# A state-space recurrence with the shared expert's matmuls between its units: x1 is turned four units earlier, and the last shared block gets a plan of its own

## The chip, the cores and the metric

The kernel runs on one core of a Trainium2 chip. The metric is the device time in microseconds (us), the median of three runs. On this core TensorE (PE) multiplies matrices into PSUM, VectorE (DVE), ScalarE (ACT) and GpSimd (POOL) work elementwise, and SyncE (SP) issues most DMAs.

## The reference

The input x is 4096 tokens by 512 channels. Two sublayers follow each other, each with a layer norm before it and one after it, and a residual.

```python
xp = x @ W_x;  dt = softplus(xp[:, :64] @ W_dt + b_dt);  B, C = xp[:, 64:80], xp[:, 80:96]
h  = exp(dt * A) * h + (dt * x) * B          # per token, 512 channels x 16 states
y  = sum_n(h * C) + x * D_skip
x1 = x + layernorm(y)
# second sublayer, on xt = layernorm(x1): top 2 of 8 experts with a capacity, and a shared expert
sh = gelu(xt @ sw1 + sb1) @ sw2 + sb2 + gelu(xt @ swd) @ swu
out = x1 + layernorm(sum_k(weight_k * expert_k(xt)) + 0.2 * sh)
```

## The kernel before

There are three program blocks, one after another: `prepare` (norm of x, dt and the B and C tables), `mix` (the recurrence, x1, and the shared expert for most tokens), and `experts` (router, gathered experts, the last 512 tokens of the shared expert, the final norm). The change touches `mix` alone.

**Units and chunks.** `mix` cuts the tokens in 8 chunks of 512 (`NCH`). A chunk has 64 units (`NU`): 4 slices of 128 channels by 16 states. A unit g is a 128x512 step on every engine: POOL makes u = dt*x*B (`drive`, line 897), ACT makes exp(dt*A) in a PSUM bank (`decay`, 646, after the one-column copy `keep`, 635), DVE runs the scan over 512 tokens (`recur`, 790) and multiplies by C (`weigh`, 797), PE adds the product, turned, into `psY` (`add`, 1014; `add_skip`, 1022, at the end of a slice, whose sum ACT takes out with `take`, 655). From unit 117 on only two PSUM banks serve the decays, so ACT makes the decay of unit g+2 in its iteration g, after the product of unit g. POOL's u runs up to six units ahead, and the products may lie five units ahead of PE.

**What is laid between the units.** When a chunk is over, its y is normed and x is added by two DMAs (`norm`, 659, units 5 to 8 of the next chunk; `residual`, 922, units 8 and 10), which gives x1. Then DVE takes the statistics of x1 (unit 16), POOL the inverse deviation (17), ACT norms four tiles (`norm_x1`, 667), SP stores them (`store_xt`, 573). PE turns each tile (`turn`, 1033) into the PSUM bank `psH`, ACT rounds it (`x_hi`, 676), DVE makes the rest (`x_lo`, 822), and each turn waits for the rest of the tile before. Then the shared expert of these 512 tokens, block b: 17 W1 blocks (`up`, 1050, twelve matmuls each; number 0 is the low-rank and router part), each taken out of the one bank `psH` by ACT two units later (`hidden_out`, 691), four bursts of gelu (`gelus`, 700, with a change of ACT's table before and after), `h_hi` (ACT, 715) and `h_lo` (POOL, 906), and 17 W2 blocks (`down`, 1071, twelve matmuls; number 0 has four, line 1061) into four PSUM banks, which DVE empties (`shared_out`, 841).

**What sets the order.** The order is a table of units, written out by hand. `due(b, unit)` gives the unit of the whole run at which a step of block b is issued; each engine walks over all units g and issues what is due, in program order, and semaphores hold the data together. A block's plan is longer than a chunk: W1 blocks at units 37, 40, ... 85 and W2 blocks at units 59 to 112, so units 0 to 21 of a chunk have W1 blocks of the block before, units 1 to 48 its W2 blocks. The recurrence has 512 units and block 6, the last in it, starts in the last chunk; what is due after unit 63 of that chunk runs without a recurrence beside it, and so do the turns and block 0 of W1 for the last 512 tokens. POOL issues the load of W1 block j+3 four units after W1 block j (950), and W2 likewise (959).

Of the kernel before, what the change touches and what calls it, by code (L numbers as in the profile page):

```python
# [36 lines left out]
FC = FF // P  # L37
# [327 lines left out]
BT = 4  # L365
FB = T // (BT * P) - 1
L3 = 3 * LR
T_AT, X_HI_AT, X_LO_AT = (24, 27, 31, 34), (25, 29, 32, 35), (27, 31, 34, 37)
UP_AT = tuple(37 + 3 * j for j in range(J))
BURST_AT = (52, 64, 77, 90)  # L370
HI_AT = (56, 58, 68, 74, 83, 88, 94, 101)
LO_AT = (59, 62, 71, 77, 86, 93, 98, 104)
LOW_HI_AT, LOW_LO_AT = 55, 58
DOWN_AT = (59, 62, 65, 68, 71, 74, 78, 81, 84, 87, 90, 94, 97, 99, 102, 106, 112)
OUT_AT = 119
B_FREE, C_FREE = 45, 51
FIRST = min(T_AT)
END = (NCH + 1) * NU
# [5 lines left out]
def due(b, unit):  # L384

    return (b + 1) * NU + unit


def mix(nc, sem, const, early, x, dt_d, dtx_d, bc_d, xT_d, w, ws_d, lgT_d, x1_d, xt_d, sh_d):
# [6 lines left out]
    with ExitStack() as ctx:  # L396
# [129 lines left out]
        @block.sync  # L526
        def _(sp):
            def next_pass(s):
                after(sp, s_yc, s - 1)
                load_pass(sp, dt_d, dtx_d, early, s)  # L530

            def next_skip(s):
                after(sp, s_yc, s)
                load_skip(sp, xT_d, early, s)

            def used(c, j):
                return (c - 1) * NU + (DT - 1) * NS + (j + 1) * TG

            def next_B(c, j):
                sp.wait_ge(s_u, used(c, j))  # L540
                load_table(sp, bc_d, Bt, s_B, 0, j, c)

            def next_C(c, j):
                sp.wait_ge(s_pd, used(c, j))
                load_table(sp, bc_d, Ct, s_C, NS, j, c)

            def load_raw(i):
                after(sp, s_wl, i - 3)
                if i < FC // 2:
                    f = 2 * i * P  # L550
                    sp.dma_start(raw_columns(i), w["sw1"].rearrange("(a p) f -> p a f", p=P)[:, :, f:f + 2 * P])\
                        .then_inc(s_wr[i % 4], 16)
                else:
                    r = (2 * i - FC) * P
                    sp.dma_start(raw_pair(i), w["sw2"][r:r + 2 * P, :].rearrange("(o p) d -> p o d", p=P))\
                        .then_inc(s_wr[i % 4], 16)

            def store_lo(i):
                sp.wait_ge(s_wl, i + 1)
                sp.dma_start(split_rows(i, 1), halves(hl, i).bitcast(F32)).then_inc(s_wls[i % 2], 16)  # L560

            def rows(a, c, t):
                return a[c * CH + t * P:c * CH + (t + 1) * P, :]

            def store_x1(c):
                for o in range(2):
                    sp.wait_ge(s_x1[o], (c + 1) * 16)
                sp.dma_start(x1_d[c * CH:(c + 1) * CH, :].rearrange("(t p) d -> p t d", p=P), ys[c % 2][:, :, :])\
                    .then_inc(s_out, 16)

            def store_xt(b, t):
                sp.wait_ge(s_xn, b * BT + t + 1)
                sp.dma_start(rows(xt_d, b, t), xn[t % 2][:, :]).then_inc(s_xt[t % 2], 16)

            def store_sh(b, t):
                sp.wait_ge(s_yev, b * BT + t + 1)
                sp.dma_start(rows(sh_d, b, t), yst[t][:, :]).then_inc(s_sh[t], 16)

            def store_logits(b):
                sp.wait_ge(s_ev, b * J + 1)  # L580
                sp.dma_start(lgT_d[:, b * CH:(b + 1) * CH], g0[L3:L3 + E, :]).then_inc(s_lgs, 16)

            sp.dma_start(wd_raw, w["swd"].rearrange("(a p) n -> p a n", p=P)).then_inc(s_stat, 16)
            sp.dma_start(gate_raw, w["gate"].rearrange("(a p) e -> p a e", p=P)).then_inc(s_stat, 16)
            for k in range(3):
                sp.dma_start(wu_raw[k * LR:(k + 1) * LR, :], w["swu"]).then_inc(s_stat, 16)
            for i in range(4):
                load_raw(i)
            sp.dma_start(b2bc[:, :], w["sb2"].partition_broadcast(P)).then_inc(s_bias, 16)
            for g in range(END):  # L590
                c, k = g // NU, g % NU
                if g == 40:
                    with nc.allow_non_contiguous_dma(reason="2048 biases"):
                        sp.dma_start(b1T[:, :], w["sb1"].rearrange("(c p) -> p c", p=P)).then_inc(s_bias, 16)
                if g == 20:
                    sp.wait_ge(early["s_last"][0], NCH // 2 * 16)
                    sp.wait_ge(early["s_last"][1], NCH // 2 * 16)
                if g % SPLIT == 0 and 0 < g // SPLIT <= FC:
                    store_lo(g // SPLIT - 1)
                    if g // SPLIT + 3 < FC:  # L600
                        load_raw(g // SPLIT + 3)
                if g % NS == 2 and 0 < g // NS < PASSES - 1:
                    next_pass(g // NS + 1)
                if g % NS == 4 and 0 < g // NS < PASSES:
                    next_skip(g // NS)
                for j in range(NG):
                    if c + 1 < NCH and k == B_FREE + 2 * j:
                        next_B(c + 1, j)
                    if 0 < g - C_FREE - 2 * j < UNITS - NU and (g - C_FREE - 2 * j) % NU == 0 or g == C_FREE + 2 * j:
                        next_C((g - C_FREE - 2 * j) // NU + 1, j)  # L610
                if c > 0:
                    if k == 16:
                        store_x1(c - 1)
                    if k in (20, 23, 29, 32):
                        store_xt(c - 1, (20, 23, 29, 32).index(k))
                for b in blocks(g):
                    for t in range(BT):
                        if due(b, OUT_AT) + 1 + t == g:
                            store_sh(b, t)
                for b in turned(g):  # L620
                    if due(b, UP_AT[0]) + 4 == g:
                        store_logits(b)
            sp.wait_ge(s_out, 16 * NCH)
            for q in range(2):
                sp.wait_ge(s_xt[q], (FB + 1) * BT // 2 * 16)
            for t in range(BT):
                sp.wait_ge(s_sh[t], FB * 16)
            sp.wait_ge(s_lgs, (FB + 1) * 16)

        @block.scalar  # L630
        def _(act):
# [106 lines left out]
            for g in range(END):  # L738
# [16 lines left out]
                if c > 0:  # L755
                    if k in (5, 6, 7, 8):
                        norm(c - 1, k - 5)
                    if k in (18, 21, 27, 30):
                        norm_x1(c - 1, (18, 21, 27, 30).index(k))
                for b in turned(g):  # L760
                    for t in range(BT):
                        if due(b, X_HI_AT[t]) == g:
                            x_hi(b, t)
                    if due(b, UP_AT[0]) + 2 == g:
                        hidden_out(b, 0)
                for b in blocks(g):
                    for j in range(1, J):
                        if due(b, UP_AT[j]) + 2 == g:
                            hidden_out(b, j)
                    for q in range(4):  # L770
                        if due(b, BURST_AT[q]) == g:
                            gelus(b, q)
                    if due(b, LOW_HI_AT) == g:
                        low_rank_hi(b)
                    for i in range(FC // 2):
                        if due(b, HI_AT[i]) == g:
                            h_hi(b, 2 * i + 1)

        @block.vector
        def _(dve):  # L780
# [75 lines left out]
            for g in range(END):  # L856
# [5 lines left out]
                        if due(b, X_LO_AT[t]) == g:  # L862
                            x_lo(b, t)
                for b in blocks(g):
                    if due(b, OUT_AT) == g:
                        for t in range(BT):
                            shared_out(b, t)
                    if due(b, LOW_LO_AT) == g:
# [20 lines left out]
        def _(pool):  # L889
# [70 lines left out]
                                    ws_d[FC + n % FC, :, :, :].rearrange("p h x -> p (h x)")).then_inc(s_w2[k], 16)  # L960

            def free_w1(n):
                return due((n - W1_RING) // FC, UP_AT[(n - W1_RING) % FC + 1]) + 4

            def free_w2(n):
                return due((n - W2_RING) // FC, DOWN_AT[(n - W2_RING) % FC + 1]) + 4

            def load_first():
                pool.wait_ge(s_yc, PASSES)
# [10 lines left out]
            for g in range(END):  # L980
# [5 lines left out]
                for b in blocks(g):  # L986
                    for i in range(FC // 2):
                        for o in range(2):
                            if due(b, LO_AT[i]) + o == g:
                                h_lo(b, 2 * i + 1 + o)  # L990
                if c > 0 and k == 4:
                    inverse(c - 1)
# [14 lines left out]
        def _(pe):  # L1007
# [68 lines left out]
            for g in range(END):  # L1076
# [4 lines left out]
                for b in turned(g):  # L1081
                    for t in range(BT):
                        if due(b, T_AT[t]) == g:
                            turn(b, t)
                    if due(b, UP_AT[0]) == g:
                        up(b, 0)
                for b in blocks(g):
                    for j in range(J):
                        if j > 0 and due(b, UP_AT[j]) == g:
                            up(b, j)  # L1090
                        if due(b, DOWN_AT[j]) == g:
                            down(b, j)


# [1143 lines left out]
```

## Time and profile before

| | |
|---|---|
| median of three runs | 3402.59 us (3400.78 to 3402.65) |
| span of the profiled execution | 3388.4 us |
| around the span (median less span) | 14.2 us |
| first scan of the recurrence | 151.7 us from the span's start |
| last product of the recurrence | 1306.4 us |
| last matmul of `mix` | ends 1377.9 us |

The profile is of one execution. Its span goes from the first to the last instruction; its own device time is not listed apart from the runs, so the span is put beside their median. PE is busy for 91% of it. The recurrence fills 151.7 to 1306.4 us; a chunk takes 146.7 to 149.8 us from chunk 2 on. 1306.4 to 1377.9 is the tail of `mix`, in which the shared expert's blocks that are left run alone; `experts` follows to the end. Times in the text are us from the span's start unless said otherwise.

### The profile page before, as it was taken

The page shows a single profiled execution, that of the slowest core. Times are in us where ns is not written, and L with a number is a line of the kernel's source. Part 1 is how long each engine was busy: PE and PEld are TensorE (multiplying, and loading weights), DVE is VectorE, ACT ScalarE, POOL GpSimd, SP SyncE. Part 2 cuts the span into 40 slices and gives each one's busy share as a digit, 9 for nine tenths or more (in the row PEclk, how much of TensorE's full clock was granted, in tenths as well). Part 3 has the DMA queues.
Part 4 walks back from the last instruction along what each step waited for, and adds up shares of the span by engine and source line. Part 5 has one row for each costly group of instructions (what it writes and reads, how often), then busy time and mean ns, then how long its engine had stood idle before and what let it go on. Part 6 is the DMA issues. An engine that isn't in the chain of part 4 may idle for free.

```text
span 3388.4 us, 42962 instructions
## 1 busy us (share of the span) xinstructions
PE 3100.0 (91%) x15139; PEld 2538.6 (75%) x15139; DVE 1812.1 (53%) x2476; ACT 1633.6 (48%) x2978; POOL 1384.2 (41%) x1367
## 2 busy tenths in 40 slices
PE   6464799988989899999999999999999999999997
PEld 3243677777767777788888888888888888888886
DVE  7797989988998984441331332322313313313345
ACT  7654676666767665452332432433423424324343
POOL 2297787988988785311110121021111111211224
PEclk9655899999999999999999999999999999999999
DMA  7968678696977865930320420412312303204355
GB/s 265 303 189 250 163 229 217 203 268 183 257 192 225 230 190 186 288 95 19 88 69 13 106 60 16 119 37 54 97 20 75 78 16 100 63 10 115 75 184 161
DMA packets 273447, 466.30 MB, mean 138 GB/s; under 512 B 30817, under 2 KB 102193, under 8 KB 273234
## 3 DMA queue, kind: packets, MB, share of 16 engines
q1 hardware_dynamic: 200400, 264.91, 26.5%
q0 software_dynamic: 66720, 189.87, 21.3%
q10 hardware_dynamic: 6114, 8.79, 0.7%
q8 instruction: 121, 1.98, 0.2%
q14 instruction: 92, 0.75, 0.1%
HBM read 366.33 MB, written 97.16 MB: 137 GB/s over the span
## 4 chain that ended last, share of the span: by engine, by line
PE 53%; DMA 2%; DVE 2%; issue 1%; ACT 1%; POOL 0%; SPq 0%; POOLq 0%; DVEq 0%; ACTq 0%
PE c_psH L2030 26%; PE c_psY L2071 25%; PE c_psT L2021 1%; DMA out<-d_y 1%; PE c_psY L2067 0%; DVE yst L1734 0%; DMA raw<-in_w 0%; DMA W2l<-ws_d 0%; DVE hl L1754 0%; ACT h L1487 0%; DVE hl L1759 0%; DVE wgt L1923 0%; PE c_psT L2130 0%; DVE hh L1753 0%; DMA d_x1p<-x_d 0%
## 5 line engine op out<-in xcount | busy, mean ns | idle before, releaser
L1759 DVE TENSOR_TENSOR hl<-h,hh 128x512 fp32r<-128x512 f32 (+1 forms) x400 | 242.5, 606 | 1185.3 <-ACT hh L1491 1185.2
L1489 ACT ACTIVATE h<-c_psH,biases 128x512 f32<-128x512 f32 (+1 forms) x400 | 248.1, 620 | 1045.0 <-PE c_psH L2030 1033.0
L897 POOL TENSOR_TENSOR u<-dtxs,Bt 128x512 f32<-128x512 f32 x512 | 669.3, 1348 | 148.2 <-DVE b_psA L790 132.9
L790 DVE TENSOR_TENSOR_SCAN b_psA<-b_psA,b_few,u 128x512 f32<-128x512 f32 x473 | 606.4, 1282 | 75.0 <-ACT b_psA L646 74.0
L2071 PE MATMUL c_psY<-W2h,hh 128*128 128x512 f32 x1344 | 535.2, 398 | 1.8 <-DVE hl L1759 1.1
L1014 PE MATMUL b_psY<-ident,pr 128*128 128x128 f32 x2048 | 345.7, 308 | 208.2 <-DVE pr L797 190.1
L2071 PE MATMUL c_psY<-W2l,hh 128*128 128x512 f32 x1344 | 525.4, 391 | 0.0
L2071 PE MATMUL c_psY<-W2h,hl 128*128 128x512 f32 x1344 | 524.4, 390 | 0.0
L1567 POOL DMA_INDIRECT xrow<-xt_d,slot_lists x80 | 84.7, 1059 | 1050.3 <-PE c_psT L2021 600.2
L1014 PEld LDWEIGHTS b_psY<-ident,pr 128*128 128x128 f32 x2048 | 265.9, 156 | 290.8 <-DVE pr L797 238.7
L646 ACT ACTIVATE b_psA<-dts,wgt 128x512 f32<-128x512 f32 x473 | 327.4, 692 | 14.9 <-ACT b_few L635 0.2
L797 DVE TENSOR_TENSOR pr<-b_psA,Ct 128x512 f32<-128x512 f32 x473 | 325.5, 688 | 14.4 <-DMA Ct<-bc_d 0.7
L1050 PE MATMUL b_psH<-Xh,w 128*128 128x512 f32 x896 | 316.7, 415 | 9.9 <-DMA w<-ws_d 9.7
L1607 POOL DMA_INDIRECT acc_d<-yst,slot_lists x72 | 117.4, 1630 | 442.7 <-DVE yst L1734 425.3
L2071 PEld LDWEIGHTS c_psY<-W2h,hl 128*128 128x128 f32 x1344 | 252.8, 188 | 54.9
L2071 PEld LDWEIGHTS c_psY<-W2h,hh 128*128 128x128 f32 x1344 | 253.2, 188 | 53.2 <-DVE hl L1759 6.2
L1071 PE MATMUL b_psS<-w,hhs 128*128 128x512 f32 x896 | 292.7, 408 | 0.0
L2071 PEld LDWEIGHTS c_psY<-W2l,hh 128*128 128x128 f32 x1344 | 253.5, 189 | 46.6 <-issue 0.2
L1491 ACT ACTIVATE hh<-c_psH,biases 128x512 fp32r<-128x512 f32 (+1 forms) x400 | 245.1, 613 | 0.0
L2030 PE MATMUL c_psH<-Xh,W1h 128*128 128x512 f32 x576 | 224.5, 390 | 0.7 <-DMA W2l<-ws_d 0.7
L2030 PE MATMUL c_psH<-Xl,W1h 128*128 128x512 f32 x576 | 224.3, 389 | 0.0
L2030 PE MATMUL c_psH<-Xh,W1l 128*128 128x512 f32 x576 | 224.2, 389 | 0.0
(271 smaller groups left out, 5685.1 us busy)
## 6 DMA issues: line engine op xcount, KB each, us to landing
w<-ws_d POOLq DMA_DIRECT2D x224, 512.0 KB, 6.6
raw<-in_w SPq DMA_DIRECT2D x256, 256.0 KB, 2.8
Bt<-bc_d SPq DMA_DIRECT2D x64, 512.0 KB, 14.6
Ct<-bc_d SPq DMA_DIRECT2D x64, 512.0 KB, 19.1
xn<-in_x SPq DMA_DIRECT2D x8, 1024.0 KB, 7.9
xT_d<-xnT SPq DMA_DIRECT2D x8, 1024.0 KB, 12.5
dt_d<-a_dt SPq DMA_DIRECT2D x8, 1024.0 KB, 8.5
dtx_d<-a_dx SPq DMA_DIRECT2D x8, 1024.0 KB, 8.7
```

The source lines that it names most:

```text
L646: nc.scalar.activation(bank(g)[:, :], dts[s % 2][:, :], ACT.Exp, scale=A_neg[:, s % DT, n:n + 1]).then_inc(s_dA, 1)
L790: nc.vector.tensor_tensor_scan(a[:, :], a[:, :], u[g % U_RING][:, :], carry[:, k:k + 1], ALU.mult, ALU.add).then_inc(s_h, 1)
L797: nc.vector.tensor_tensor(pr[g % PR_RING][:, :], bank(g)[:, :], C_of(g), ALU.mult)\
L897: nc.gpsimd.tensor_tensor(u[g % U_RING][:, :], dtx[s % 2][:, :], Bt[n // TG][:, n % TG, :], ALU.mult)\
L1014: last = nc.tensor.matmul(psY[:, t, :], pr[g % PR_RING][:, t * P:(t + 1) * P], ident[:, :], start=(n == 0 and t == 0), stop=False, is_tran ...
L1050: last = nc.tensor.matmul(out, a[:, d, :], v[:, d, :], start=(d == 0 and i == 0), stop=(d == DT - 1 and i == 2))
L1071: last = nc.tensor.matmul(psS[t][:, :], a, v, start=False, stop=(j == FC and i == 2))
L1489: nc.scalar.activation(h32[:, 0:n * P], psH[j % 2][:, 0:n * P], ACT.Gelu, bias=b1[:, j - 1:j])
L1491: nc.scalar.activation(hh[j % 2][:, 0:n * P], psH[j % 2][:, 0:n * P], ACT.Gelu, bias=b1[:, j - 1:j]).then_inc(s_gelu, 1)
L1759: nc.vector.tensor_tensor(hl[j % 2][a], h32[a], hh[j % 2][a].bitcast(F32), ALU.subtract)\
L2030: last = nc.tensor.matmul(out, a, b, start=(i == 0), stop=(i == n - 1))
L2071: last = nc.tensor.matmul(psY[t][:, :], a[j % 2][:, c], b, start=False, stop=(j == J - 1 and i == 2))
```

## The change

The turns of x1 move from units 24, 27, 31, 34 to 20, 23, 27, 30, `x_hi` and `x_lo` with them by four units. The norms before them move from 18, 21, 27, 30 to 18, 20, 23, 26 and the stores from 20, 23, 29, 32 to 19, 22, 25, 28. W1 blocks start at unit 34 instead of 37, still every three units, so their units are the same ones with one more at 34 and none at 85 (unit 21 of the next chunk). Bursts, `h_hi`, `h_lo`, W2 blocks and the output keep their units. Block 6 gets a plan of its own, `FINAL`.

```diff
-T_AT, X_HI_AT, X_LO_AT = (24, 27, 31, 34), (25, 29, 32, 35), (27, 31, 34, 37)
-UP_AT = tuple(37 + 3 * j for j in range(J))
-BURST_AT = (52, 64, 77, 90)
-HI_AT = (56, 58, 68, 74, 83, 88, 94, 101)
-LO_AT = (59, 62, 71, 77, 86, 93, 98, 104)
+T_AT, X_HI_AT, X_LO_AT = (20, 23, 27, 30), (21, 25, 28, 31), (23, 27, 30, 33)
+X1_NORM_AT, XT_STORE_AT = (18, 20, 23, 26), (19, 22, 25, 28)
 LOW_HI_AT, LOW_LO_AT = 55, 58
-DOWN_AT = (59, 62, 65, 68, 71, 74, 78, 81, 84, 87, 90, 94, 97, 99, 102, 106, 112)
-OUT_AT = 119
+USUAL = dict(
+    up=tuple(34 + 3 * j for j in range(J)), burst=(52, 64, 77, 90), hi=(56, 58, 68, 74, 83, 88, 94, 101),
+    lo=(59, 62, 71, 77, 86, 93, 98, 104),
+    down=(59, 62, 65, 68, 71, 74, 78, 81, 84, 87, 90, 94, 97, 99, 102, 106, 112), out=119)
+FINAL = dict(
+    up=(34, 37, 40, 43, 46, 48, 50, 52, 54, 56, 58, 60, 62, 68, 70, 74, 77), burst=(51, 57, 65, 81),
+    hi=(54, 58, 67, 71, 76, 81, 86, 91), lo=(57, 61, 69, 74, 78, 83, 88, 93),
+    down=(62, 64, 66, 68, 70, 73, 75, 78, 80, 83, 85, 88, 90, 92, 94, 97, 99), out=102)
...
+def plan(b):
+
+    return FINAL if b == FB - 1 else USUAL
```

Everywhere else `UP_AT`, `BURST_AT` and so on become `plan(b)["up"]`, `plan(b)["burst"]`. No instruction is added or taken away; the order on each queue changes.

## Rows read from the trace of the kernel before

**Rows 1.** Part 1 of the page: busy us (share of the span) xinstructions
```profile
PE 3100.0 (91%) x15139; PEld 2538.6 (75%) x15139; DVE 1812.1 (53%) x2476; ACT 1633.6 (48%) x2978; POOL 1384.2 (41%) x1367
```
**Rows 2.** Busy time by stretch: chunk 5, chunk 7, tail of mix
```profile
core 0: us, PE busy (x) PEld busy (x) DVE busy (x) ACT busy (x) POOL busy (x), PEclk, DMA share, GB/s
863.84:1010.86 147.02, 133.17 (x707) 110.14 (x707) 133.44 (x155) 99.89 (x187) 124.69 (x123) 0.95 0.80 221
...
1157.55:1306.36 148.81, 133.69 (x713) 110.79 (x712) 133.60 (x154) 99.46 (x186) 121.42 (x120) 0.97 0.62 188
1306.36:1377.90 71.54, 71.53 (x329) 58.66 (x327) 10.58 (x23) 27.99 (x36) 33.26 (x43) 1.00 0.65 202
```
**Rows 3.** Waits within chunk 5: total us, times, longest
```profile
PE b_psY L1014 <- DVE pr L797: 11.2, 9, 4.5
DVE b_psA L790 <- ACT b_psA L646: 7.9, 6, 2.3
```
**Rows 4.** DVE in order of time, chunk 5: start, us, instruction, [idle before]
```profile
918.00 1.29 DVE L790 TENSOR_TENSOR_SCAN b_psA<-b_psA,b_few,u 128x512 f32<-128x512 f32 x1 [0.96 <-ACT b_psA L646]
...
919.93 1.28 DVE L790 TENSOR_TENSOR_SCAN b_psA<-b_psA,b_few,u 128x512 f32<-128x512 f32 x1
...
924.83 1.29 DVE L790 TENSOR_TENSOR_SCAN b_psA<-b_psA,b_few,u 128x512 f32<-128x512 f32 x1 [0.96 <-ACT b_psA L646]
...
928.44 0.69 DVE L822 TENSOR_TENSOR Xl<-b_psH,Xh 128x512 fp32r<-128x512 f32 x1 [1.59 <-ACT Xh L676]
929.04 1.28 DVE L790 TENSOR_TENSOR_SCAN b_psA<-b_psA,b_few,u 128x512 f32<-128x512 f32 x1
...
934.59 1.29 DVE L790 TENSOR_TENSOR_SCAN b_psA<-b_psA,b_few,u 128x512 f32<-128x512 f32 x1 [1.62 <-ACT b_psA L646]
...
945.94 0.69 DVE L822 TENSOR_TENSOR Xl<-b_psH,Xh 128x512 fp32r<-128x512 f32 x1 [1.03 <-ACT Xh L676]
...
986.34 1.29 DVE L790 TENSOR_TENSOR_SCAN b_psA<-b_psA,b_few,u 128x512 f32<-128x512 f32 x1 [0.62 <-ACT b_psA L646]
...
992.22 1.29 DVE L790 TENSOR_TENSOR_SCAN b_psA<-b_psA,b_few,u 128x512 f32<-128x512 f32 x1 [1.48 <-ACT b_psA L646]
```
**Rows 5.** ACT in order of time, around the burst of unit 26
```profile
929.21 1.28 ACT L700 ACT_TABLE_LOAD   x1
930.50 2.01 ACT L700 ACTIVATE hb<-hb 128x1024 f32<-128x1024 f32 x2
...
933.87 0.69 ACT L646 ACTIVATE b_psA<-dts,wgt 128x512 f32<-128x512 f32 x1
934.50 0.80 ACT L667 ACTIVATE xn<-ys,b_few 128x512 f32<-128x512 f32 x1
```
**Rows 6.** PE in order of time, units 30 to 56 of chunk 5
```profile
938.59 1.12 PE L1014 MATMUL b_psY<-ident,pr 128*128 128x128 f32 x4 [0.81 <-DVE pr L797]
...
950.53 0.66 PE L1014 MATMUL b_psY<-ident,pr 128*128 128x128 f32 x4 [0.34 <-DVE pr L797]
...
954.98 0.66 PE L1014 MATMUL b_psY<-ident,pr 128*128 128x128 f32 x4 [0.61 <-DVE pr L797]
955.39 0.47 PE L1050 MATMUL b_psH<-Xh,L1h 128*104 128x512 f32 x1
...
958.25 0.60 PE L1014 MATMUL b_psY<-ident,pr 128*128 128x128 f32 x4
...
994.30 1.11 PE L1014 MATMUL b_psY<-ident,pr 128*128 128x128 f32 x4 [4.52 <-DVE pr L797]
```
**Rows 7.** Busy time and granted clock of shorter stretches, columns as in rows 2
```profile
934.90:941.60 6.70, 4.12 (x13) 3.29 (x14) 6.60 (x8) 5.41 (x12) 5.51 (x5) 0.50 0.37 122
941.70:985.60 43.90, 42.03 (x237) 34.99 (x236) 42.12 (x46) 23.28 (x52) 37.08 (x35) 1.00 0.59 172
...
1281.30:1310.30 29.00, 22.76 (x120) 18.65 (x117) 22.72 (x25) 18.03 (x31) 14.56 (x14) 0.94 0.40 127
```
**Rows 8.** The same view for the tail from unit 64's W1 block on
```profile
1310.30:1377.70 67.40, 67.40 (x307) 55.29 (x305) 10.38 (x23) 27.63 (x35) 32.22 (x41) 1.00 0.66 205
```
**Rows 9.** POOL in order of time: second residual DMA of the tail
```profile
1323.42 1.74 POOL L922 DMA_DIRECT2D ys<-in_x  x1
```
**Rows 10.** ACT in order of time: first norm of x1 in the tail
```profile
1341.12 0.80 ACT L667 ACTIVATE xn<-ys,b_few 128x512 f32<-128x512 f32 x1
```
**Rows 11.** PE in order of time: first turn of the tail
```profile
1353.93 0.60 PE L1033 MATMUL b_psH<-ident,xn 128*128 128x128 f32 x4
```

More of the change, by code:

```diff
@@ L613, in _ @@
                         store_x1(c - 1)
-                    if k in (20, 23, 29, 32):
-                        store_xt(c - 1, (20, 23, 29, 32).index(k))
+                    if k in XT_STORE_AT:
+                        store_xt(c - 1, XT_STORE_AT.index(k))
                 for b in blocks(g):
                     for t in range(BT):
-                        if due(b, OUT_AT) + 1 + t == g:
+                        if due(b, plan(b)["out"]) + 1 + t == g:
                             store_sh(b, t)
                 for b in turned(g):
-                    if due(b, UP_AT[0]) + 4 == g:
+                    if due(b, plan(b)["up"][0]) + 4 == g:
                         store_logits(b)
@@ L757, in _ @@
                         norm(c - 1, k - 5)
-                    if k in (18, 21, 27, 30):
-                        norm_x1(c - 1, (18, 21, 27, 30).index(k))
+                    if k in X1_NORM_AT:
+                        norm_x1(c - 1, X1_NORM_AT.index(k))
                 for b in turned(g):
@@ L763, in _ @@
                             x_hi(b, t)
-                    if due(b, UP_AT[0]) + 2 == g:
+                    if due(b, plan(b)["up"][0]) + 2 == g:
                         hidden_out(b, 0)
@@ L767, in _ @@
                     for j in range(1, J):
-                        if due(b, UP_AT[j]) + 2 == g:
+                        if due(b, plan(b)["up"][j]) + 2 == g:
                             hidden_out(b, j)
                     for q in range(4):
-                        if due(b, BURST_AT[q]) == g:
+                        if due(b, plan(b)["burst"][q]) == g:
                             gelus(b, q)
@@ L775, in _ @@
                     for i in range(FC // 2):
-                        if due(b, HI_AT[i]) == g:
+                        if due(b, plan(b)["hi"][i]) == g:
                             h_hi(b, 2 * i + 1)
@@ L864, in _ @@
                 for b in blocks(g):
-                    if due(b, OUT_AT) == g:
+                    if due(b, plan(b)["out"]) == g:
                         for t in range(BT):
@@ L962, in free_w1 @@
             def free_w1(n):
-                return due((n - W1_RING) // FC, UP_AT[(n - W1_RING) % FC + 1]) + 4
+                b, j = (n - W1_RING) // FC, (n - W1_RING) % FC + 1
+                return due(b, plan(b)["up"][j]) + 4
             def free_w2(n):
-                return due((n - W2_RING) // FC, DOWN_AT[(n - W2_RING) % FC + 1]) + 4
+                b, j = (n - W2_RING) // FC, (n - W2_RING) % FC + 1
+                return due(b, plan(b)["down"][j]) + 4
             def load_first():
@@ L988, in _ @@
                         for o in range(2):
-                            if due(b, LO_AT[i]) + o == g:
+                            if due(b, plan(b)["lo"][i]) + o == g:
                                 h_lo(b, 2 * i + 1 + o)
@@ L1084, in _ @@
                             turn(b, t)
-                    if due(b, UP_AT[0]) == g:
+                    if due(b, plan(b)["up"][0]) == g:
                         up(b, 0)
@@ L1088, in _ @@
                     for j in range(J):
-                        if j > 0 and due(b, UP_AT[j]) == g:
+                        if j > 0 and due(b, plan(b)["up"][j]) == g:
                             up(b, j)
-                        if due(b, DOWN_AT[j]) == g:
+                        if due(b, plan(b)["down"][j]) == g:
                             down(b, j)
```

## The prediction

> **What bounds the kernel now.** I read the busy shares first, then the stages, then the waits of one chunk, then single queues around the moved steps. PE is busy for 91% of the span and DVE for 53% [rows 1], but the change lies in the recurrence, where both are near full: in chunk 5 each has some 133 us of 147.02 [rows 2]. Two scans follow each other in 1.93 us [rows 4], so 64 units need 123.5 us; the rest is other DVE work and idle time. The idle time is divided: DVE waits 7.9 us for ACT's decays, and PE waits 11.2 us for DVE's products [rows 3]. So neither is the bound throughout; they take turns. After the recurrence the tail is PE alone: 71.53 us busy of 71.54 [rows 2]. `experts` starts when `mix` ends, so its part of the span should only shift.
>
> Chunks 2 to 6 show the same pattern, so I price chunk 5 and multiply by five; chunks 1 and 7 and the tail are taken apart.
>
> **Turns four units earlier, up to unit 30.** Before, DVE loses 0.96 us twice (918.00, 924.83: the scans of units 23 and 26 wait for decays that stand behind an eviction of a late W1 block), 1.59 us at the first `x_lo` (928.44), 1.62 us at scan 29 and 1.03 us at the third `x_lo` [rows 4]. That is 6.2 us, the largest prize in sight. Walked through with the new order:
> - The first `x_lo` now stands before scan 23. Its turn comes behind the W1 block of unit 18, whose eviction ends at about 917.2; turn 0.6 after that, `x_hi` to 918.6, `x_lo` (0.6 net) to 919.2. Scan 23 starts at 919.2 instead of 918.00.
> - No W1 block at unit 21: the 0.96 at scan 26 goes. Scan 26 starts at 919.2 + 3 x 1.93 = 925.0, before at 924.83. The second `x_lo` is due next, its turn long done: 0.6 without a wait, where 1.59 + 0.6 stood before. Product 26 ends at 927.0.
> - The gelu burst of unit 26 now decides. ACT: one-column copy and decay 0.9 (0.69 of it the decay), the fourth norm 0.80 (new at this place), table and gelu from 929.21 to 932.5 = 3.3, table and decay to 934.56 = 2.05 [rows 5]. 927.0 + 7.1 = 934.1 for scan 29, before 934.59. The 1.62 us of waiting grows to some 2.6.
> - The third `x_lo` now before scan 30, 0.6: product 30 ends at about 938.65. Before, PE's add of unit 30 started at 938.59 [rows 6], at once on that product.
>
> So DVE has done two more `x_lo` by then and has lost nothing; freed of the 1.03 us wait it would be 1.9 us ahead at unit 38 (2 x 0.6 + 1.03, less 0.1, and rounding).
>
> **The W1 block at 34.** The block that left unit 21 comes back at unit 34, on the far side of the burst. Is there room on PE? From the add of unit 30 (938.59) to the fourth W2 block from there (unit 38, which follows the add at 958.25 by 0.35) PE takes 20.0 us. It idles 0.34 and 0.61 us before adds [rows 6], some 0.5 more around these, and runs at the half clock (granted 0.50, the 1.2 GHz level) till 941.7, after waiting for DVE through the burst [rows 7]. New content: one more block, 955.39 to 958.25 = 2.86 us [rows 6]; one turn less (hidden in the wait for `take`, so worth nothing); the last turn moved into the half-clock stretch, +0.4; idle time used up, -1.5; the rest rounding. 2.86 + 0.4 - 1.5 - 0.1 = **+1.6 us**. From unit 38 on the order is the old one, and from 941.70 to 985.60 PE is busy 42.03 of 43.90 us [rows 7]: no room to win it back. DVE's lead of 1.9 us is spent in evictions: ACT waits for late W1 blocks at 42, 45, 51 and the decays behind them come late. The old kernel shows this at one place already, 0.62 us at scan 54 [rows 4]. Behind scan 54 stands the next burst, PE idles 4.52 us [rows 6] and starts afresh: what is late at scan 54 stays late for the chunk. Ends: -1.9 (the lead is kept) and +3.3 (the half clock lasts through the W2 block of unit 30). I take +1.6, since PE's rows there have no gap: 5 x 1.6 = **+8.0**.
>
> Chunk 1 has no W2 blocks in this part and a PE with gaps, so it keeps the wait at the third `x_lo`: **-0.8** (between 0 and -1.9).
>
> **The last block's plan.** In chunk 7, W1 blocks come every two units from 46, so 13 instead of 9 lie before unit 64, and one W2 block instead of two: three blocks leave the tail. The tail's 67.40 us hold 24 blocks and four turns of 0.4 [rows 8], so 2.74 per block: -8.2. What they cost in chunk 7:
> - PE from unit 33 to 51 is as late as in the other chunks and full (+0.6 at its start, +1.6 at unit 38).
> - The burst moves to unit 51, with the eviction of the W1 block of unit 50 behind it. With one PSUM bank for all W1 blocks PE can't begin the one of unit 52 before: it idles about 3.9 us, in place of 4.52 at units 54 to 56. DVE waits too, and its four `shared_out` (2.56 us) at 55 no longer hide in that wait, as they do between 986.34 and 992.22 [rows 4].
> - The second burst, 64 before and so in the tail beside PE's work, is now at 57, inside the recurrence: 3.3 for gelu and 1.3 for the table of exp are laid on ACT's queue ahead of a decay and an eviction. DVE loses about 2.7 us and PE 3.6.
>
> Walked on unit by unit with 1.93 per unit, 0.9 per decay, 0.7 per eviction, 2.86 per block, the last skip matmuls end at 1319.1 instead of 1310.3: +8.8. Together with -8.2 that is +0.6. PE has three gaps of 2 to 4 us in that stretch where it had one of 4.52 and one of 1.2; the stretch before had a granted clock of 0.94 [rows 7], and at the half clock a block takes up to twice its 2.86. I add 1.5, half a block: **+2.1**, between -8.2 (all hidden) and +6.
>
> In the tail `h_hi` of unit 71 waits for the W2 block of unit 70 and stands before the fourth norm and, through `h_lo`, before the second residual DMA. That one went out at 1323.42, 17 us after the last product [rows 9]; I get 1338 to 1339. x1's first norm was at 1341.12 [rows 10] and its turn at 1353.93 [rows 11], 12 us of slack. Now the norm is at about 1353.5 and the turn, 13 blocks after 1319.1, at 1354.6. It just holds; I cost it at nothing, and each us by which it is missed is one of the tail.
>
> **Sum.** 8.0 - 0.8 + 2.1 = +9.3 us. On the profiled execution: span 3388.4 + 9.3 = 3397.7, with 14.2 around it 3411.9. The median of the runs is 3402.59, which is the same sum, so **3412 us**.
>
> **Rivals.**
> 1. *PE has room for the block at 34.* Then DVE's lead stays: 5 x -1.9 = -9.5, with -0.8 and +2.1 3402.6 - 8.2 = 3394. For it: from 941.70 to 985.60 weight loads take 34.99 us of 43.90, 80% [rows 7]. Against it: they take 55.29 of 67.40 in the tail, 82%, where PE has no gap at all [rows 8], so 80% is full. The Trainium skill, "Perfetto Trace Analysis", section "Identifying the Most-Contended Engine", says to judge TensorE's headroom by MFU and the busy share of LDWEIGHTS and not by matmul occupancy; read that way a fifth of the stretch would be free and this rival would hold. Chance 0.15.
> 2. *The last plan pays.* The three gaps of chunk 7 coincide with waits PE had anyway, say because ACT's burst runs while PE is still behind. Then chunk 7 and the tail give -6 instead of +2.1: 3403.8; with a chunk price of 1.0 instead of 1.6 3400.8. For it: PE idles 6.2 of 29 us there [rows 7]. Against it: each gap follows from one bank and one queue. Chance 0.20.
> 3. *x1 comes late in the tail.* The fourth norm behind `h_hi` delays the turns so that PE stands, and the half clock follows: from 12 us of lateness used up, each us more counts fully; with a DMA 5 us slower, and one block after it at the half clock, +8: 3420. For it: the slack falls from 12 to 1 us. Chance 0.10.
>
> The forecast has 0.55. A measurement of this kernel tells 0.2%, 6.8 us, from no change. The forecast's own range is 3406 to 3418, of which about a fifth lies inside 0.2%. Slower: 0.43 + 0.10 = 0.53; same: 0.12 + 0.13 of rival 2 = 0.25; faster: 0.15 + 0.07 = 0.22. Range for 8 in 10: 3393 to 3423, from rival 1 to rival 3.
>
> **What would show it.** Scan 23 starts later after 22 than before (wait at `x_lo` about 1.7) and scan 26 without a wait; the norm before the burst's table load; product 30 at the same distance from the chunk's start as before; no gap on PE between units 31 and 52, and waits of 1 us at scans near 42, 45, 48 and 54; chunks 2 to 6 longer by 1.6 each. In chunk 7 PE gaps at 52 and 58, recurrence's end 8 us later in the chunk, a tail some 8 us shorter. Wrong would be: chunks 2 to 6 shorter than before (rival 1), or chunk 7 with tail shorter by over 4 us (rival 2).

## The result, and the profile after

The changed kernel takes 3407.67 us (median of 6 runs, 3404.45 to 3409.78), the kernel before 3400.47 us beside it (6 runs). The ratio is 1.0026, 95% interval 1.0016 to 1.0036 (that of the two medians is 1.0021): slower by 5 to 12 us. The forecast was 3412 us, +9.3 us.

Part 1 of the page of the kernel after, to be read beside [rows 1]: every engine has the same work as before, so the time is in the waits.

```profile
PE 3104.0 (91%) x15139; PEld 2541.0 (75%) x15139; DVE 1814.4 (53%) x2476; ACT 1636.2 (48%) x2980; POOL 1385.0 (41%) x1367
```

The busy time by stretch of the kernel after (columns as in [rows 2]): chunk 5, chunk 7, units 17 to 31 and 31 to 54 of chunk 5, and the tail from the last skip matmuls on.

```profile
868.55:1019.12 150.57, 135.29 (x712) 112.06 (x711) 133.89 (x155) 99.97 (x187) 124.82 (x123) 0.95 0.80 218
1168.93:1324.43 155.50, 138.97 (x719) 114.55 (x718) 134.59 (x154) 104.38 (x191) 122.42 (x121) 0.95 0.63 187
...
911.78:944.94 33.16, 26.82 (x153) 22.14 (x151) 28.48 (x32) 24.23 (x44) 30.85 (x33) 0.96 0.66 212
944.94:994.60 49.66, 48.16 (x258) 40.60 (x259) 44.66 (x49) 26.00 (x58) 41.12 (x39) 0.96 0.63 180
1330.33:1395.00 64.67, 60.40 (x271) 48.43 (x269) 10.57 (x23) 23.93 (x30) 30.30 (x38) 1.00 0.61 190
```

The same stretch 31 to 54 of chunk 5 of the kernel before:

```profile
939.05:986.34 47.29, 45.42 (x250) 37.85 (x249) 44.85 (x49) 26.60 (x58) 40.34 (x38) 0.97 0.60 175
```

PE's busy time in it grows from 45.42 to 48.16 us, one block's 2.74, and the stretch from 47.29 to 49.66: the block that came back at unit 34 is paid nearly in full. In the tail the reader is to see the opposite: 64.67 us with 60.40 busy, where [rows 8] has 67.40 of 67.40. Three blocks have left, and a part of the room they left is idle.

DVE in order of time, chunk 5 of the kernel after, to be read beside [rows 4]:

```profile
925.04 0.69 DVE L830 TENSOR_TENSOR Xl<-b_psH,Xh 128x512 fp32r<-128x512 f32 x1 [1.58 <-ACT Xh L684]
...
940.49 1.29 DVE L798 TENSOR_TENSOR_SCAN b_psA<-b_psA,b_few,u 128x512 f32<-128x512 f32 x1 [2.61 <-ACT b_psA L654]
942.42 0.68 DVE L830 TENSOR_TENSOR Xl<-b_psH,Xh 128x512 fp32r<-128x512 f32 x1
...
968.20 1.29 DVE L798 TENSOR_TENSOR_SCAN b_psA<-b_psA,b_few,u 128x512 f32<-128x512 f32 x1 [1.03 <-ACT b_psA L654]
975.03 1.29 DVE L798 TENSOR_TENSOR_SCAN b_psA<-b_psA,b_few,u 128x512 f32<-128x512 f32 x1 [0.96 <-ACT b_psA L654]
981.85 1.29 DVE L798 TENSOR_TENSOR_SCAN b_psA<-b_psA,b_few,u 128x512 f32<-128x512 f32 x1 [0.96 <-ACT b_psA L654]
994.60 1.29 DVE L798 TENSOR_TENSOR_SCAN b_psA<-b_psA,b_few,u 128x512 f32<-128x512 f32 x1 [0.97 <-ACT b_psA L654]
```

The waits went where the walk put them: 1.58 at the first `x_lo` (between scans 22 and 23 now), 2.61 at scan 29, none at the third `x_lo`, and then a wait of about 1 us at scans 42, 45, 48 and 54.

PE in order of time, the gaps of chunk 7 and of the tail of the kernel after:

```profile
1299.94 0.50 PE L1060 MATMUL b_psH<-Xh,w 128*128 128x512 f32 x1 [3.36 <-ACT hb L699]
...
1313.36 0.66 PE L1024 MATMUL b_psY<-ident,pr 128*128 128x128 f32 x4 [0.73 <-DVE pr L805]
1316.43 0.50 PE L1060 MATMUL b_psH<-Xh,w 128*128 128x512 f32 x1 [2.41 <-ACT hb L699]
...
1349.22 0.70 PE L1081 MATMUL b_psS<-w,hhs 128*128 128x512 f32 x2 [2.28 <-DMA w<-ws_d]
1373.42 0.70 PE L1081 MATMUL b_psS<-w,hhs 128*128 128x512 f32 x2 [1.22 <-DMA w<-ws_d]
1386.51 0.70 PE L1081 MATMUL b_psS<-w,hhs 128*128 128x512 f32 x2 [0.78 <-DMA w<-ws_d]
```

The first and third are W1 blocks that wait for the eviction (`hb`) behind a gelu burst, as forecast. The last three, 4.3 us, were not: W2 blocks that wait for their weights.

Where the time went between the two profiled executions, worked out from the starts of the scans and PE's rows (us):

| | before | after | change | forecast |
|---|---|---|---|---|
| start and chunk 0 | 272.1 | 272.6 | +0.5 | 0 |
| chunk 1 | 147.26 | 147.91 | +0.65 | -0.8 |
| chunks 2 to 6 | 738.2 | 748.4 | +10.2 | +8.0 |
| chunk 7 to the last skip matmuls | 152.7 | 161.4 | +8.7 | +8.8 and +1.5 |
| from there to the end of `mix` | 67.6 | 64.7 | -2.9 | -8.2 |
| `experts` | 2010.5 | 2010.5 | 0.0 | 0 |

That is 17.1 us between two executions, where the medians differ by 7.2: an execution scatters by some 10 us, and before's profiled one lay at the low end. So the table tells where things are, and the ratio how much it is.

### The profile page after: what moved, and what is told of

It reads as the page before. It is cut to its first block, busy times and chain, and to the rows that moved or that the text cites. A ratio compares the mean times of both kernels' runs of the same rounds, so it can differ in the third digit from the quotient of the medians.

```text
span 3405.5 us, 42964 instructions
## 1 busy us (share of the span) xinstructions
PE 3104.0 (91%) x15139; PEld 2541.0 (75%) x15139; DVE 1814.4 (53%) x2476; ACT 1636.2 (48%) x2980; POOL 1385.0 (41%) x1367
## 4 chain that ended last, share of the span: by engine, by line
PE 53%; DVE 2%; DMA 2%; issue 1%; ACT 1%; SPq 0%; POOL 0%; POOLq 0%; DVEq 0%; ACTq 0%
PE c_psH L2040 26%; PE c_psY L2081 25%; PE c_psT L2031 1%; DMA out<-d_y 1%; DMA raw<-in_w 1%; PE c_psY L2077 1%; DVE yst L1744 0%; DVE hl L1764 0%; ACT h L1497 0%; DVE hl L1769 0%; PE c_psT L2140 0%; ACT h L1499 0%; DVE hh L1763 0%; DMA d_x1p<-x_d 0%; DVE wgt L1933 0%
```

## The experiments

Twelve kernels, in three groups of four, each beside the kernel before on its chip (median 3392 to 3393 us there).

**The kernel before once more,** as a control.

> The kernel before, unchanged, for a second trace: its profiled execution (span 3388.4 us) lies some 10 us under the median of the runs, the one of the changed kernel (3405.5) does not. If the difference is in waits for DMAs, the stretch from unit 17 to unit 54 of chunks 2 to 6 is again 80.5 us on the mean and units 54 to 64 again 24.5, and what differs lies in units 0 to 17, before the recurrence or after mix. If the first trace was fast for another reason, the stretch from 17 to 54 is longer too, say by 1 us, and my price of the early turns is too high by that.

3392.85 us, span 3390.9; chunk 5 takes 147.02, chunks 2 to 6 148.4 in the mean (147.6 in the first profile). Units 17 to 54 are steadier than whole chunks: 80.5 and 81.0 in the mean of chunks 2 to 6. They are what I compare from here on.

**Early turns without the last plan.**

```diff
-    return FINAL if b == FB - 1 else USUAL
+    return USUAL
```

> The early turns and the W1 blocks from 34 on, for all blocks; the last block has the plan of the others. PE theory: in chunks 2 to 7 the stretch from unit 17 to unit 54 takes 82.3 us instead of 80.5, chunk 1's 0.9 less. In chunk 7 the block that comes back at 34 is one less in the tail (2.7). Sum 6 x 1.85 - 0.9 - 2.7 = +7.5 us, ratio 1.002. Rival, the cost is all in the last block's plan: the stretch as before, ratio 1.000 or under.

3394.14 us, ratio 1.0002 (0.9993 to 1.0011). Units 17 to 54 take 82.2 us, as in the kernel after (82.3), so the +1.6 per chunk is there in this stretch (+1.2 to +1.8). But the whole is hardly slower. In its profile units 0 to 17 are 1.1 to 1.3 us shorter per chunk than in the two of before, chunk 1's units 17 to 54 are 0.9 to 1.3 us shorter, and of the block fewer in the tail nothing is gained, since turns now wait there. PE, tail of early_only:

```profile
1347.17 0.63 PE L1043 MATMUL b_psH<-ident,xn 128*128 128x128 f32 x4 [0.87 <-ACT hb L699]
...
1358.40 0.63 PE L1043 MATMUL b_psH<-ident,xn 128*128 128x128 f32 x4 [1.49 <-DVE Xl L830]
```

I expected a price here that the runs didn't show.

**The last plan without the early turns.** Turns, norms, stores and the usual plan as before; in the last block:

```diff
-    up=(34, 37, 40, 43, 46, 48, 50, 52, 54, 56, 58, 60, 62, 68, 70, 74, 77), burst=(51, 57, 65, 81),
+    up=(37, 40, 43, 46, 48, 50, 52, 54, 56, 58, 60, 62, 65, 68, 70, 74, 77), burst=(51, 59, 67, 81),
```

> Turns, norms, stores and W1 blocks of all blocks as before (W1 from 37), the last block alone with the new plan; its W1 blocks are 37, 40, 43, 46, 48 and then every two units to 62, then 65, 68, 70, 74, 77, its bursts 51, 59, 67, 81. Chunks 1 to 6 as before. In chunk 7 the second burst is still inside the recurrence and PE has two gaps behind the bursts: recurrence 5 to 7 us longer than before, tail with 22 blocks for 24 (5.5 less) plus about 5 of waits for W2 loads. Sum +4 to +7 us, ratio 1.0015. Rival, the last plan pays and the early turns cost all: ratio 0.9985 to 1.000, chunk 7 and tail together under 220.4 us.

3407.62 us, ratio 1.0045 (1.0031 to 1.0059). Chunk 7 takes 154.30 us against 148.1 to 148.8, and the time from the last product to the end of `mix` grows from 71.5 to 79.8, with fewer blocks in it. PE in order of time, the gaps of the tail of final_only:

```profile
1340.98 1.19 PE L1081 MATMUL b_psS<-w,hhs 128*128 128x512 f32 x2 [2.85 <-DMA w<-ws_d]
1368.28 0.70 PE L1081 MATMUL b_psS<-w,hhs 128*128 128x512 f32 x2 [1.94 <-DMA w<-ws_d]
1381.93 0.70 PE L1081 MATMUL b_psS<-w,hhs 128*128 128x512 f32 x2 [1.57 <-DMA w<-ws_d]
```

The last plan alone makes the kernel slower, and its tail waits for W2 weights here too.

**The second burst back at 64,** where it no longer stands before decays.

```diff
-    ... burst=(51, 57, 65, 81),
+    ... burst=(51, 64, 65, 81),
```

> The changed kernel with the second burst of the last block at unit 64 instead of 57, so behind the recurrence. If that burst costs what I reckoned, the PE gap of 2.4 us before the W1 block of unit 60 goes and the recurrence in chunk 7 ends 3 to 4 us earlier than in the changed kernel (155.5 us), the tail stays at 70.6 or grows by what ACT is late there, at most 1: mix 2 to 4 us shorter, ratio to before 1.001 to 1.002. Rival, DVE and PE lose nothing by the burst since PE is the bound in the whole of chunk 7: chunk 7 within 0.5 us of 155.5.

3399.30 us, ratio 1.0018 (1.0009 to 1.0028). Units 54 to 64 of chunk 7 take 23.64 us instead of 25.11, and the gap of 2.41 us on PE falls to 0.86:

```profile
1296.37 0.72 PE L1060 MATMUL b_psH<-Xh,w 128*128 128x512 f32 x1 [3.36 <-ACT hb L699]
1309.81 0.66 PE L1024 MATMUL b_psY<-ident,pr 128*128 128x128 f32 x4 [0.73 <-DVE pr L805]
1311.33 0.50 PE L1060 MATMUL b_psH<-Xh,w 128*128 128x512 f32 x1 [0.86 <-ACT hb L699]
```

Chunk 7 is 1.6 us shorter than in the kernel after and the rest of `mix` 1.1. So the burst inside the recurrence costs about 2.7 us. From scan 31 of chunk 7 to the last skip matmuls alone, without the units 0 to 17 that scatter, it takes 84.0 us here and 86.5 to 87.9 in the four kernels with the same last plan and the burst at 57: 2.5 to 3.9.

**One W1 block twice, at two places.** The kernel before, with the twelve matmuls of one W1 block done twice (the second run overwrites the first with the same sums): that of unit 37 (`j == 0`), and that of unit 55 (`j == 6`).

```diff
-                for d in range(DT):
+                for again in range(2 if j == 0 and b < FB else 1):
+                  for d in range(DT):
```

> The kernel before, with the matmuls of W1 block 0 (unit 37) done twice in each shared block but the last: one extra block of PE work (2.86 us in the profile of before) in the stretch of units 31 to 54 of chunks 1 to 7. Theory (PE has no room there): units 31 to 54 grow by 2.3 to 2.9 us per chunk, about 16 to 20 us in all, 3409 to 3413 on this chip. Rival (PE's weight loads leave a fifth of the stretch free): under 0.5 us per chunk, 3393 to 3397.

> The kernel before, with the matmuls of W1 block 6 (unit 55) done twice instead: the same work, but laid beside the 4.5 us in which PE waits behind the gelu burst. Theory (there is room at this place alone): 0 to 1 us per chunk, 3393 to 3400. Rival (PE is the bound of the whole chunk): the same 16 to 20 us as when the first block is doubled.

The first: 3404.60 us, ratio 1.0031 (1.0020 to 1.0043). The second: 3392.70 us, 1.0001 (0.9992 to 1.0011). Units 31 to 54 and then 54 to 64 of chunk 5, the block of unit 37 doubled:

```profile
950.56:1001.59 51.03, 49.19 (x262) 40.59 (x261) 45.18 (x49) 26.40 (x58) 40.55 (x38) 0.95 0.59 169
1001.59:1026.12 24.53, 18.23 (x90) 14.45 (x89) 22.64 (x25) 17.78 (x31) 16.41 (x16) 0.93 0.98 229
```

and the block of unit 55 doubled:

```profile
940.76:988.80 48.04, 46.23 (x250) 38.44 (x249) 44.84 (x49) 26.60 (x58) 41.67 (x40) 0.95 0.60 173
988.80:1013.56 24.76, 20.00 (x100) 16.48 (x99) 22.75 (x26) 17.57 (x31) 16.64 (x16) 0.93 0.94 238
```

In the mean of chunks 2 to 6 units 31 to 54 take 50.7 us with the first, against 47.3 and 47.9 in the two profiles of before: +2.8 to +3.4 for 2.86 us of matmuls. With the second they take 47.9, and units 54 to 64 25.6 instead of 24.5. The same work costs its full length in the one stretch and a third of it in the other. PE has no room between units 31 and 54, and this decides against rival 1. `mix` as a whole ends 18 to 20 us later with the first, as expected; the median grows only by 12, partly because `experts` took 2006.9 us with both doubled kernels and 2009.0 to 2012.4 with the others. Why, stays open.

**Early turns with PE's gap filled.** W1 blocks from 37 again, the one left over beside PE's wait behind the burst.

```diff
-    up=tuple(34 + 3 * j for j in range(J)), burst=(52, 64, 77, 90), ...
+    up=(37, 40, 43, 46, 49, 52, 55, 57, 59, 61, 64, 67, 70, 73, 76, 79, 82), burst=(52, 64, 77, 90), ...
```

> Turns, norms and stores as after, usual plan in every block, but W1 blocks again from unit 37 and the one left over at unit 59 of a row 55, 57, 59, 61, 64, that is beside PE's wait behind the burst. Theory (DVE's lead of the early turns is lost only to the block at unit 34): units 17 to 54 shorter than before by about 1.9 us per chunk, 3381 to 3388. Rival (the blocks two units apart after the burst delay decays by as much): 3390 to 3397, no gain.

3418.61 us, ratio 1.0079 (1.0064 to 1.0093): the slowest of all, where I expected the fastest. Units 17 to 54 do get shorter, to 79.5 us: by 1.0, not the 1.9 of the prediction's lead, against 80.5 in the mean of the profiles with late turns. But units 0 to 4 go from 12.5 to 19.2 us. PE in order of time, about the end of chunk 2:

```profile
569.46 0.47 PE L1060 MATMUL b_psH<-Xh,w 128*128 128x512 f32 x1 [1.98 <-DMA w<-ws_d]
577.52 0.48 PE L1060 MATMUL b_psH<-Xh,w 128*128 128x512 f32 x1 [4.18 <-DMA w<-ws_d]
```

and how long the W1 loads of this stretch take from issue to landing, this kernel and then the kernel before:

```profile
DMA to landing us min/median/max: 7.4/11.3/13.5
```

```profile
DMA to landing us min/median/max: 7.3/12.1/14.3
```

A load takes 11 to 12 us here in either kernel, six units. It is issued four units after a W1 block and wanted at the third block behind it: five units are left to it with blocks three apart, some 9.7 us, and two with blocks two apart. So it can't land in time. ACT waits 7.4 us for that block, and a decay behind it keeps DVE 5.7 us. The room on PE was real, the room on the DMA queues was not.

**Three versions of the tail's loads.** Two things stood near the W2 waits: the two loads for `experts` (`load_first`, at unit 6 of the tail; 512 KB each in the trace, where my expectations say 1 MB) and the four units between a W2 block and the load into its tile. The first version moves both:

```diff
-                return due(b, plan(b)["down"][j]) + 4
+                return due(b, plan(b)["down"][j]) + (4 if b < FB - 1 else 1)
...
-                if g == UNITS + 6:
+                if g == UNITS + 20:
```

> The kernel after, with the last shared block's W2 loads issued one unit after the block that frees the tile (not four), and the two 1 MB loads for the experts at 20 units after the last scan, not 6. Theory (the tail's missing 5 us are PE's waits for W2): the tail shortens by 4 to 5 us against after, ratio to before about 1.0012. Rival (the waits come from the DMA queues' own load, whatever the issue time): tail as after, within 1 us, ratio 1.0026.

3403.61 us, ratio 1.0032 (1.0019 to 1.0044): no gain. PE's rows have no gap up to 1361 us, and then a W2 block waits behind the other loads' new place, which went out at 1359.1 and 1359.9:

```profile
1367.48 0.70 PE L1081 MATMUL b_psS<-w,hhs 128*128 128x512 f32 x2 [2.91 <-DMA w<-ws_d]
```

So I moved the loads for `experts` behind all others (`UNITS + 38`), once with the four units kept and once with one.

> The kernel after, with the two 1 MB loads for the experts issued behind all W2 loads of the tail (38 units after the last scan, not 6). Theory (the tail's missing 5 us are W2 loads that share the queues with these two): tail from the last skip matmuls 60 to 61.5 us instead of 64.7; what comes after mix may grow by 0 to 4 us. Rival (POOL's order and the 4 units between a block and its load make the wait): tail as after, within 1 us.

> As prefetch_last, and the W2 loads of the last block issued one unit after the block that frees their tile, not four. Theory: no W2 wait left in the tail, 22 blocks and four turns in 60 us from the last skip matmuls. Rival (loads sooner bring nothing once the two large loads are gone): the same tail as prefetch_last.

3402.88 us, ratio 1.0028 (1.0017 to 1.0039), and 3397.61 us, ratio 1.0017 (1.0007 to 1.0026). The tail from the last skip matmuls on, with the same 271 matmul records as after's row above, in loads_sooner, prefetch_last and prefetch_last_loads_sooner:

```profile
1322.49:1386.70 64.21, 61.30 (x271) 49.61 (x269) 10.57 (x23) 24.04 (x30) 30.97 (x39) 0.97 0.64 191
```

```profile
1326.72:1389.90 63.18, 59.98 (x271) 48.50 (x269) 10.59 (x23) 23.94 (x30) 30.32 (x38) 1.00 0.65 195
```

```profile
1328.83:1388.29 59.46, 59.46 (x271) 48.53 (x269) 10.58 (x23) 24.05 (x30) 30.91 (x39) 1.00 0.70 207
```

64.67 with neither, 64.21 with early W2 loads and those for `experts` in between, 63.18 with the latter last, 59.46 with both: only both together take the waits away, and then PE is busy for all of it. Early W2 loads with those for `experts` left at unit 6 were not run. How long the W2 loads of this tail take from issue to landing, in the kernel after and with both changes:

```profile
DMA to landing us min/median/max: 3.5/4.4/10.5
```

```profile
DMA to landing us min/median/max: 3.4/4.3/7.7
```

The median is the same; the few long ones and the late issue made the waits: the block at 1349.22 in the kernel after waited for a load that took 7.8 us beside those for `experts`, the ones at 1373.42 and 1386.51 for loads that took 3.75 and 3.55 us and went out 3.9 and 3.7 us before. I had expected the loads for `experts` alone to do it and was wrong. `experts` takes 2010.5 us with its loads issued last, as before, so that costs nothing there.

**A W2 block out of the full stretch.** If a block costs 2.9 us in units 31 to 54 and less ahead of them, the early turns should be followed by W2 blocks that move ahead. From early_only:

```diff
-    ... hi=(56, 58, 68, 74, 83, 88, 94, 101), lo=(59, 62, 71, 77, 86, 93, 98, 104),
-    down=(59, 62, 65, 68, 71, 74, 78, 81, 84, 87, 90, 94, 97, 99, 102, 106, 112), out=119)
+    ... hi=(56, 58, 68, 74, 82, 86, 94, 101), lo=(59, 62, 71, 77, 84, 89, 98, 104),
+    down=(59, 62, 65, 68, 71, 74, 78, 81, 84, 86, 88, 91, 94, 99, 102, 106, 112), out=119)
```

> The early turns with the usual plan in every block (as early_only), and in each block the W2 blocks of units 87, 90, 94, 97 at 86, 88, 91, 94: so four instead of five of them lie between units 31 and 54 of the next chunk, and six instead of five between 17 and 31. Theory (a block costs its 2.9 us in units 31 to 54, where PE has no room, and less before the burst of unit 26, where PE waits): units 17 to 54 at 79.5 to 80.5 us instead of 82.2 (early_only) or 80.5 to 81.0 (before); 3376 to 3386. Rival (PE is as full in 17 to 31, the block only moves): 82, and 3391 to 3396.

3382.71 us, ratio 0.9975 (0.9964 to 0.9985), faster than both kernels. Units 17 to 31 and 31 to 54 of chunk 5:

```profile
900.98:933.74 32.76, 28.79 (x162) 23.79 (x160) 28.54 (x32) 24.17 (x44) 29.94 (x32) 0.97 0.65 206
933.74:980.92 47.18, 45.69 (x246) 38.59 (x247) 44.44 (x49) 26.33 (x58) 40.49 (x39) 0.95 0.60 170
```

Against after's two rows PE is busy 2.0 us more in the first, which is 0.4 us shorter, and 2.5 us less in the second, which is 2.5 us shorter. In the mean of chunks 2 to 6 units 17 to 54 take 79.4 us, 2.8 less than early_only. The `h_hi` and `h_lo` steps that feed these blocks move by one to four units with them, and what they do alone wasn't run.

**The fourth burst three units sooner as well.**

```diff
-    ... burst=(52, 64, 77, 90), hi=(..., 94, 101), lo=(..., 98, 104),
-    down=(..., 94, 99, 102, 106, 112), out=119)
+    ... burst=(52, 64, 77, 87), hi=(..., 91, 97), lo=(..., 94, 101),
+    down=(..., 94, 97, 101, 105, 111), out=119)
```

> As w2_pulled, and the fourth burst at unit 87 (23 of the next chunk) instead of 90, since its last W1 block is now at 82; the last six W2 blocks one to three units sooner. Theory: as w2_pulled and PE has three more units after the burst's wait before the full stretch: units 17 to 54 at 79 to 80.5 us; 3374 to 3386. Rival (the burst stands too close to the evictions of the W1 blocks at 18 and 21 and to the turns at 20 and 23, whose x_lo then wait): 81 to 83, and 3390 to 3397.

3381.08 us, ratio 0.9964 (0.9954 to 0.9974), 12 us faster than the kernel before. The two stretches of chunk 5 again:

```profile
906.13:940.80 34.67, 27.93 (x140) 23.11 (x140) 28.44 (x33) 25.24 (x45) 34.16 (x36) 0.90 0.69 206
940.80:986.19 45.39, 44.71 (x258) 38.06 (x257) 44.17 (x48) 25.72 (x57) 38.98 (x38) 1.00 0.62 170
```

The burst's move takes 1.8 us from units 31 to 54 and gives 1.9 to units 17 to 31, where DVE now waits 3.35 us behind it. The sum is that of w2_pulled (79.7 and 79.4), and the two intervals overlap: the gain is that of the W2 blocks, and nothing shows that the burst adds to it.

## Why the prediction was right, and the step that was not

- **Turns and the waits of units 17 to 31: right.** The wait at `x_lo` forecast as 1.7 us is 1.58, the one at scan 29 forecast as 2.6 is 2.61, and the waits of 1 us at 23 and 26 and at the third `x_lo` are gone. Units 17 to 54 of chunk 1 fall from 69.08 to 68.15 us (forecast -0.8). The lead that these turns would give alone was too high: forecast as 1.9 us (its own terms add up to 2.0), 1.0 in early_gap_filled.
- **The W1 block at 34: right.** Forecast +1.6 per chunk; units 17 to 54 take 82.0 to 83.3 us (mean of chunks 2 to 6) in the kernel after and the five others with its turns and usual plan, 82.5 in their mean, and 80.1 to 81.0, 80.5 in the mean, in four profiles without (before, twice, final_only, double_late): +1.9. Against the 79.5 of early_gap_filled, with the early turns and no block at 34, it is 3.0, the whole block. The doubled block shows the cause. The Trainium skill, "Perfetto Trace Analysis", section "Identifying the Most-Contended Engine", would judge PE's headroom by MFU and the busy share of its weight loads, and not by its matmuls' busy share. Here the weight loads are busy 37.85 of 47.29 us, 80%, and an added block still cost its whole length: the measurement decides, and PE was full, as its matmuls' 45.42 of 47.29 us (96%) say.
- **Chunk 7: right.** +8.7 us against +8.8, or against +10.3 with the half block at the lower clock (+1.5) that I added for its gaps. The mean granted clock of chunk 7 falls from 0.97 to 0.95; the +8.7 holds what that costs, and no run prices it by itself. Gaps of 3.36 us before the block at 52 and 2.41 us before the one at 60 (I had written 58) stand in PE's rows. The burst's share, "DVE loses about 2.7 us and PE 3.6", is 2.7 us when it is moved away.
- **The tail: mis-sized.** "Three blocks leave the tail ... -8.2" is a bound and not what came: -2.9. I priced a block by the rows of a tail in which W1 and W2 blocks alternate, so that a W2 tile had two blocks' time to be filled. With the W1 blocks gone the W2 blocks follow each other in 2.72 us, and loads that take 3.5 to 10.5 us come late. With the loads mended the tail is 59.46 us against 67.40: -7.9, my term. The step that failed is the overlap: I put PE's waits for W2 loads at nothing without a reason, and they take 4.3 us in the kernel after.
- **x1 in the tail: right.** The first norm starts at 1366.88 and its turn at 1368.39, 38 us after the last skip matmuls, and PE doesn't wait for it; rival 3 didn't come.
- **The sum: right in size, by errors that cancel, which is luck.** The runs gave +1 us (-2 to +4) for the early turns alone, where my terms make +6 (+8.0 - 0.8, 1.6 more for chunk 7, and 2.7 less for the block that leaves the tail). The profiles show more of it: whole chunks 2 to 6 take 149.0 us in the mean of the six kernels above and 147.7 in the three profiles with late turns and nothing doubled, +1.3 per chunk. Why the runs show less stays open. The last plan cost more than I said: from early_only to the kernel after the ratio goes from 1.0002 to 1.0026, 8 us, where the other terms make 3.2.
- **"14.2 around it": wrong.** The profiled run of the kernel after took 3407.54 us with a span of 3405.5, so 2.0 us lie around a span. Before's profiled execution was simply some 12 us faster than the median beside it. The number that came out was right since I took the median as the base.

**Units 0 to 17: overlooked.** They take 41.5 to 42.9 us in the six kernels and 42.1 to 42.9 in those with late turns, so whether early turns give something back there is not shown. Their length goes with another wait, that for W1 loads. Waits of the kernel before in units 0 to 17 of chunk 4 (total us, times, longest):

```profile
DVE b_psA L790 <- ACT b_psA L646: 5.5, 2, 3.6
ACT hb L691 <- PE b_psH L1050: 5.0, 1, 5.0
PE b_psH L1050 <- DMA w<-ws_d: 2.4, 1, 2.4
```

PE waits for the weights, ACT for PE's block, DVE for the decay behind its eviction. Over these units of chunks 2 to 6 PE waits for W1 loads between 2.7 us (loads_sooner, the shortest of the ten profiles there, 207.6 us) and 9.3 us (before_again, the longest, 214.5). Loads of 11 to 12 us with some 9.7 us to land fit that. It is argued from these rows and not shown: issuing the loads sooner there wasn't tried.

Rival 2 (the last plan pays) is refuted by final_only, at 1.0045, and by chunk 7 and tail together, +5.8 us in the kernel after. With burst_out's 2.7 us and the tail's 5.2 both won back it would be 8.7 - 2.7 - 7.9, a gain of some 2 us if the two add up; that combination wasn't run. Nor was the kernel before with W2 blocks pulled ahead and late turns, so how much of the 12 us needs the early turns is open.

## What to carry to other kernels

A step that is freed of its waits brings nothing if its work lands where the other engine is full: look at the stretch it leaves and the one it enters, and double a block there to price it (here 2.86 us of matmuls cost 2.8 to 3.4 us at one place and 1 us at another). When work leaves a stage in which two kinds of blocks alternate, check the loads of the kind that stays, for it now has half the time, and check the queue's latency at that place: 4 us in one stretch of this kernel, 12 us in another. What made the kernel faster was to move filler work one stretch ahead, out of the full one.

## What the runs showed of the hardware

- The latency of the same 512 KB load depends on where it is issued: 3.4 to 5.6 us in the quiet part of the tail, up to 7.7 (W2) and 8.05 us (W1) beside the residual's two loads alone (prefetch_last_loads_sooner), 7.8 to 11.0 us where those for `experts` are in flight too (the kernel after), and 12.1 us in the median at the end of chunk 2 of the kernel before, where the DMA share is 0.94 (543 to 567 us).
- After a wait of 2.85 us in the tail of final_only the granted clock fell to 0.50, the 1.2 GHz level: the block behind it took 5.26 us instead of 2.72 (its first row is 1.19 us long, 0.70 in the rows behind shorter waits). After the wait of 2.91 us in loads_sooner it fell for 3.4 us and the block took 4.42 us, and after one of 2.28 us in the kernel after it stayed at 1.00. So a wait for a load cost 0 to 2.5 us more than its own length.
